# A perceiver of four layers on one core: first head reordered, scan products in pairs, one norm for two, loads ahead in portions, tails in halves

## The reference

```python
x = x + L0_xattn(ctx, layernorm(x), mask, ...)
# L0_xattn: xn = LN(ctx)*ln_x_g + ln_x_b;  ln = LN(layernorm(x))*ln_l_g + ln_l_b
#   q = ln @ Wq;  k, v = concat(xn, ln) @ Wkv
#   qn = rmsnorm(q, qn_g)/8;  kn = rmsnorm(k, kn_g);  out = softmax(mask(qn @ kn.T)) @ v @ Wout + bout
...
x = x + L1_attn(layernorm(x), ...)
# L1_attn: xn = LN(x)*ln_g + ln_b; returns x + mamba(xn) + mamba(xn reversed) reversed
# mamba: h = exp(dt*A)*h + dt*u*B ;  y = sum_n h*C + u*D     (512 inner, 16 states)
...
x = x + L2_attn(layernorm(x), ...)   # one mamba, 256 inner, 16 states
```

## Time and profile before

| | us |
|---|---|
| runs of the kernel before (3) | 2944.35 median, 2940.78 to 2949.25 |
| the profiled execution | 2943.97, span 2942.2 |
| busy in it: PE / DVE / ACT / POOL | 2679.1 / 1659.3 / 1107.9 / 610.0 |
| mean granted TensorE clock | 0.955 of full |

### The profile page before, as it was taken

How to read it: one execution, slowest core, us unless ns; L and a number is a source line. 1 busy time by engine, 2 the same in 40 slices (tenths; PEclk the granted TensorE clock), 3 DMA queues, 4 the chain that set the end, 5 groups by cost and what they waited for, 6 DMA issues and landing times. The chain is left out here.

```text
span 2942.2 us, 44133 instructions
## 1 busy us (share of the span) xinstructions
PE 2679.1 (91%) x17647; PEld 1865.4 (63%) x17647; DVE 1659.3 (56%) x3739; ACT 1107.9 (38%) x1993; POOL 610.0 (21%) x316
## 2 busy tenths in 40 slices
PE   5899999999999999689999878998996788889978
PEld 2466666666666666456767645665993467778846
DVE  5557565666666653646566555773452260067755
ACT  2343434344343432215555536651331342211123
POOL 2040403122131400000000004771001051145402
PEclk9999999999999999899999999998998899999989
DMA  4233242333324220231010001115676438643200
GB/s 156 70 82 108 69 122 75 104 97 82 97 71 109 70 60 24 86 114 46 24 46 24 2 7 34 44 40 193 242 298 247 153 95 292 216 175 134 68 16 34
DMA packets 90545, 296.06 MB, mean 101 GB/s; under 512 B 8752, under 2 KB 46326, under 8 KB 83686
## 3 DMA queue, kind: packets, MB, share of 16 engines
q1 hardware_dynamic: 86342, 284.26, 30.2%
q0 software_dynamic: 2976, 8.13, 0.8%
q10 hardware_dynamic: 1024, 0.86, 0.1%
HBM read 281.16 MB, written 11.54 MB: 99 GB/s over the span
## 5 line engine op out<-in xcount | busy, mean ns | idle before, releaser
L1923 PE MATMUL L_xattn_bank<-L_xattn_keys_tok,L_xattn_probsT 128*128 128x257 f32 x1664 | 413.3, 392 | 1.1 <-ACT L_xattn_probsT L1740 0.2
L1852 PE MATMUL L_xattn_wide<-L_xattn_keys_feat,weights_a 128*128 128x512 f32 (+2 forms) x1024 | 388.2, 522 | 4.7 <-ACT L_xattn_keys_feat L1760 3.4
L1923 PEld LDWEIGHTS L_xattn_bank<-L_xattn_keys_tok,L_xattn_probsT 128*128 128x128 f32 x1664 | 301.1, 190 | 91.2 <-issue 40.9
L1852 PEld LDWEIGHTS L_xattn_wide<-L_xattn_keys_feat,weights_a 128*128 128x128 f32 x1024 | 186.1, 192 | 152.8 <-issue 125.4
L1509 DVE COPY L_xattn_k_normed<-L_xattn_wide 128x833 f32<-128x833 f32 (+1 forms) x128 | 131.1, 1024 | 192.4 <-PE L_xattn_wide L1852 192.2
L1734 ACT ACTIVATE L_xattn_scores<-L_xattn_scores,L_xattn_neg_max 128x897 f32<-128x897 f32 x128 | 126.4, 1035 | 256.7 <-DVE L_xattn_neg_max L1534 256.7
L2868 DVE TENSOR_TENSOR_SCAN L_attn_state<-L_attn_decay,L_attn_banks 128x1024 f32<-128x1024 f32 x80 | 182.7, 2286 | 71.1 <-PE L_attn_banks L3070 71.1
L2974 POOL TENSOR_TENSOR L_attn_state<-L_attn_state,L_attn_C_rows 128x1024 f32<-128x1024 f32 x80 | 188.7, 2360 | 71.7 <-DVE L_attn_state L2868 71.6
L1529 DVE CUSTOM_DVE_ANT_0 L_xattn_scores<-L_xattn_wide,L_xattn_mask_row 128x897 f32<-128x897 f32 x128 | 134.9, 1088 | 105.9 <-issue 105.9
L3070 PEld LDWEIGHTS L_attn_banks<-L_attn_B_diagonal,L_attn_dt_u_tok 128*128 128x128 f32 x1280 | 151.1, 194 | 66.1 <-issue 64.5
L2137 DVE CUSTOM_DVE_ANT_0 L_xattn_scores<-L_xattn_banks,L_xattn_mask 128x512 f32<-128x512 f32 (+1 forms) x256 | 131.4, 569 | 92.5 <-issue 92.5
(11 more groups left out here) (522 smaller groups left out, 4714.6 us busy)
## 6 DMA issues: line engine op xcount, KB each, us to landing
L_xattn_k_scale<-L_xattn_k_scale_rows SPq DMA_DIRECT2D x128, 417.0 KB, 5.0
L_ffn_expert_w<-in_x_L_ffn SPq DMA_DIRECT2D x16, 2056.0 KB, 9.0
L_xattn_ctx_feat<-in_ctx_feat SPq DMA_DIRECT2D x20, 1601.0 KB, 8.8
L_ffn_expert_w<-in_x_L_ffn SPq DMA_DIRECT2D x17, 1024.0 KB, 5.5
L_ffn_expert_w<-in_x_L_ffn SPq DMA_DIRECT2D x15, 1028.0 KB, 5.6
L_xattn_keys_tok<-in_ctx_tok SPq DMA_DIRECT2D x8, 1536.0 KB
L_attn_C_rows<-L_attn_c_rows SPq DMA_DIRECT2D x48, 256.0 KB, 3.3
L_xattn_ctx_tok_and_one<-in_ctx_tok SPq DMA_DIRECT2D x8, 1536.0 KB
```

The costliest lines, as they stand in the source:

```text
L1852: last = nc.tensor.matmul(wide[:, 2 * h + c, 0:n], wk[:, k, p * P:(p + 1) * P], xnT[b % 2][:, k, a:a + n], start=(k == 0), stop=(k == KT - 1))
L1923: last = nc.tensor.matmul(bS[:, 0:D + 1], pT[:, c, a, :, :].rearrange("p h q -> p (h q)"), xn[b % 2][:, t, :], start=(i == 0), stop=(i == ...
```

## The change

1. **First head.** The opening block goes. L0_xattn's SP list itself loads x, the small columns of the weights, the first 690 columns of the constants, Wq, then context 0 and mask 0, and then the rest, each with its own semaphore. The columns of the weights are packed in another order. The two norms of x become one, with 1/sqrt((1+eps)v + eps²). Gain and bias of the latents are applied while the turned tensor is copied out of PSUM; the token-layout latents are gained after the query groups. The statistics of context 0 start before the query groups, its norms come in four pieces at groups 2 to 5, and PE turns the ungained context inside groups 4 to 7; gain and bias are applied in those copies. POOL spreads mask 0 first, and gains the tokens after the latents and all eight turns. SP moves the latents behind the turns.
2. **L1_attn**: one norm for two, with the same scale; the memset and x += first norm move behind.
3. **Scan loop**: two products, then two sums.
4. **L1_ffn**: the loads ahead go out in three portions, behind load(4), load(7) and load(10).
5. **Tails**: the projection is signalled by halves, the result is added by halves, the bias earlier in the loop.

```diff
-def norm_scalar(L, act, ln_stats_ready, rstd_ready, nx=0):
+def norm_scalar(L, act, ln_stats_ready, rstd_ready, twice=False):
...
+        nc.scalar.activation(rstd, L.mv[:, 2 * h:2 * h + 2, 1], ACT.Ln, scale=1.0 + EPS if twice else 1.0,
+                             bias=L.eps[:, 1:2] if twice else L.eps[:, 0:1]).then_inc(rstd_ready, 1)
...
+                L.load_first(sp, "x")
                 load_ctx(0)
                 load_mask(0)
+                L.load_first(sp, "rest")
                 sp.wait_ge(latents_ready, 1)
                 sp.dma_start(own_rows.rearrange("(t j) d -> j t d", j=2), L.z[S - 1:P:S, :, :]).then_inc(own_stored, 16)
                 sp.wait_ge(own_stored, 16)
+                sp.wait_ge(xn_turned, 8)
...
+                ctx_stats(0, range(*CTX_PIECES[0]))
...
+                norm_after = {2: range(0, 4), 3: range(4, 7), 4: range(7, 10), 5: range(10, TILES)}
                 for p in range(NQ):
...
-                    if p in (1, 2):
-                        ctx_stats(0, range(*CTX_PIECES[p - 1]))
-                    if p in (3, 4):
-                        ctx_norm(0, range(*CTX_PIECES[p - 3]))
+                    if p == 1:
+                        ctx_stats(0, range(*CTX_PIECES[1]))
+                    if p in norm_after:
+                        ctx_norm(0, norm_after[p])
+                    if p >= TURN_AFTER:
+                        keys_turned((p - TURN_AFTER) % KT, (p - TURN_AFTER) // KT)
                 q_gained(NQ - 1)
+                dve.wait_ge(w_ready[0], w_ready[1])
+                g = lambda n: w[:, at[n]:at[n] + D].unsqueeze(1).broadcast_to([P, NT, D])
+                chain(nc.vector.tensor_tensor(L.z[:, :, :], L.z[:, :, :], g("ln_l_g"), ALU.mult))
+                nc.vector.tensor_tensor(L.z[:, :, :], L.z[:, :, :], g("ln_l_b"), ALU.add).then_inc(latents_ready, 1)
...
-                dve.wait_ge(projected, 1)
-                chain(nc.vector.tensor_tensor(L.x[:, :, :], L.x[:, :, :],
-                                              wide[:, 0:2, :].rearrange("p a (b n) -> p (a b) n", n=D), ALU.add))
-                chain(nc.vector.tensor_tensor(L.x[:, :, :], L.x[:, :, :],
-                                              w[:, at["bout"]:at["bout"] + D].unsqueeze(1).broadcast_to([P, NT, D]),
-                                              ALU.add))
+                    if s == NQ:
+                        chain(nc.vector.tensor_tensor(L.x[:, :, :], L.x[:, :, :],
+                                                      w[:, at["bout"]:at["bout"] + D].unsqueeze(1).broadcast_to([P, NT, D]),
+                                                      ALU.add))
+                for half in range(2):
+                    dve.wait_ge(projected, half + 1)
+                    nc.vector.tensor_tensor(L.x[:, 2 * half:2 * half + 2, :], L.x[:, 2 * half:2 * half + 2, :],
+                                            wide[:, half, :].rearrange("p (b n) -> p b n", n=D), ALU.add)
...
+                pool.wait_ge(mask_zeroed, 1)
+                mask_row(0)
                 pool.wait_ge(w_ready[0], w_ready[1])
+                pool.wait_ge(latents_ready, 1)
+                pool.wait_ge(xn_turned, 8)
+                pool.wait_ge(mask_ready, 2)
+                gains(0, 0)
+                gains(0, 1)
...
                 project_q(0)
                 for p in range(NQ):
                     if p + 1 < NQ:
                         project_q(p + 1)
                     mean_q(p)
+                    if p >= TURN_AFTER:
+                        turn_keys((p - TURN_AFTER) % KT, (p - TURN_AFTER) // KT)
+                pe.wait_ge(L.rest_loaded, 32)
+                pe.wait_ge(w_ready[0], w_ready[1])
...
-                norm_vector(L, dve, chain, ln_stats_ready, rstd_ready, z_ready)
-                if twice:
-                    dve.wait_ge(z_ready, 2)
-                    chain(nc.vector.tensor_tensor(L.x[:, :, :], L.x[:, :, :], L.z[:, :, :], ALU.add))
-                    norm_vector(L, dve, chain, ln_stats_ready, rstd_ready, z_ready, x=L.z, z=z2, nx=1)
+                norm_vector(L, dve, chain, ln_stats_ready, rstd_ready, z_ready, z=z2)
...
+                if twice:
+                    dve.wait_ge(first_rstd_ready, 2)
+                    for t in range(NT):
+                        last = nc.vector.tensor_scalar(L.z[:, t, :], L.x[:, t, :], L.mv[:, t, 0:1], first_rstd[:, t:t + 1],
+                                                       ALU.subtract, ALU.mult)
+                    chain(last)
+                    chain(nc.vector.tensor_tensor(L.x[:, :, :], L.x[:, :, :], L.z[:, :, :], ALU.add))
...
-                for p in range(PIECES):
-                    if p + 2 < PIECES:
-                        state_input(p + 2)
-                    if p >= SPAN and p - SPAN < PC:
-                        start_y(1, p - SPAN)
...
-                    add_state(p)
+                for first in range(0, PIECES, 2):
+                    for p in (first, first + 1):
+                        if p + 2 < PIECES:
+                            state_input(p + 2)
+                    for p in (first, first + 1):
+                        if p >= SPAN and p - SPAN < PC:
+                            start_y(1, p - SPAN)
+                    for p in (first, first + 1):
...
+                        add_state(p)
...
-    AHEAD_AT = 8
+    AHEAD_AT = (4, 7, 10)
...
-                    if shared and j == AHEAD_AT:
-                        load_l2_ahead(L, sp)
+                    if shared and j in AHEAD_AT:
+                        load_l2_ahead(L, sp, AHEAD_AT.index(j))
```

More of the change, by code:

```diff
@@ L219, in turn_tensor @@
     for h in range(2):
-        if z_ready is not None:
-            pe.wait_ge(z_ready, seen + h + 1)
+        pe.wait_ge(z_ready, h + 1)
         for k in range(KT):
@@ L1460, in _ @@
                 chain(nc.vector.memset(mv[:, :, :], 1.0))
+                dve.wait_ge(zT_turned, 2)
+                for k in range(KT):
+                    nc.vector.tensor_scalar(L.zT[:, k, N // 2:N], turned_half(wide, 1)[:, k, :],
+                                            w[:, at["ln_l_gc"] + k:at["ln_l_gc"] + k + 1],
+                                            w[:, at["ln_l_bc"] + k:at["ln_l_bc"] + k + 1], ALU.mult, ALU.add
+                                            ).then_inc(zT_ready, 1)
                 for n in range(2):
@@ L1479, in q_gained, with keys_turned @@
                                                    sc[:, (p % 2) * N:(p % 2 + 1) * N], ALU.mult, ALU.mult).then_inc(q_ready, 1)
+                def keys_turned(k, x):
+                    g = 2 * x + 1
+                    a, n = KEY_GROUPS[g]
+                    dve.wait_ge(xn_turned, 4 * x + 2 * k + 2)
+                    if x == 0:
+                        nc.vector.tensor_copy(xnT[0][:, k, FIRST:FIRST + 1], L.zT[:, k, S - 1:S])
+                    cols = sum(rows(t) for t in range(a, a + n))
+                    a = key_place(a)
+                    nc.vector.tensor_scalar(xnT[0][:, k, a:a + cols], bT[:, 1, 0:cols],
+                                            w[:, at["ln_x_gc"] + k:at["ln_x_gc"] + k + 1],
+                                            w[:, at["ln_x_bc"] + k:at["ln_x_bc"] + k + 1], ALU.mult, ALU.add
+                                            ).then_inc(xT_dve, 1)
+                norm_after = {2: range(0, 4), 3: range(4, 7), 4: range(7, 10), 5: range(10, TILES)}
                 for p in range(NQ):
@@ L1815, in mean_q, with turn_keys @@
                                      ).then_inc(q_meaned, 1)
+                def turn_keys(k, x):
+                    pe.wait_ge(ctx_normed, x + 1)
+                    for g in (2 * x, 2 * x + 1):
+                        if g % 2 == 0:
+                            pe.wait_ge(xT_act, 2 * x + k)
+                        else:
+                            pe.wait_ge(xT_dve, 2 * x + k)
+                        a, n = KEY_GROUPS[g]
+                        for i in range(n):
+                            last = nc.tensor.transpose(bT[:, g % 2, i * P:(i + 1) * P], xn[0][:, a + i, k * P:(k + 1) * P],
+                                                       L.ident)
+                        last.then_inc(xn_turned, 1)
                 project_q(0)
@@ L2163, in _ @@
                     unit_taken(i)
+                    if i == 3:
+                        chain(nc.vector.tensor_tensor(L.x[:, :, :], L.x[:, :, :],
+                                                      w[:, at["bo"]:at["bo"] + D].unsqueeze(1).broadcast_to([P, NT, D]),
+                                                      ALU.add))
                 for s in range(QUADS + 1):
@@ L2807, in _ @@
                                                 ).then_inc(zT_ready, 1)
+                if KD > R:
+                    for d in range(ND):
+                        last = nc.vector.memset(dbc[d][R:KD, :], 1.0)
+                    last.then_inc(ones_ready, 1)
                 def convolve(d, m0):
@@ L2980, in _ @@
```

(6 more changed lines are left out.)

231 lines of the change are left out of this document (107 added, 124 removed).

## The result

| | us | ratio to before (95% interval) |
|---|---|---|
| changed kernel, first chip (4 runs) | 2892.55 (2889.15 to 2896.66), before 2942.84 there | 0.9826 (0.9805 to 0.9847) |
| the same again, another chip (5 runs) | 2895.22, before 2944.96 there | 0.9835 (0.9820 to 0.9850) |
| its profiled execution | span 2891.9 | |

Faster by 50 us, 1.7%; forecast 2890, range 2880 to 2911. Where it came from is read best from block to block: TensorE's first matmul of each of the twelve blocks, in the profiled executions before and after.

The account below looks back on a forecast made before the run. TensorE was taken to bound the steps and scan loop, and the chains it waits for elsewhere. 26.1 + 5.7 + 3.5 + 13.2 + 5.6 = 54.1 off 2943.97 gave 2890 us, range 2880 to 2911.

Parts of the forecast that it names:

- Head, 26.1: Opening of L0_xattn: first keys matmul at 43.5 instead of 69.62, saving 26.1 us, bounds 19 to 29.
- (a): Opening: the queries start at 10.7, 13.3 us earlier; bounds 10 to 13.5.
- (b): Opening: six blocked context norms on DVE, 7.94 us, would take 2.1, saving 5.8; bounds 0 to 5.8.
- (c): Opening: separate context turns, 6.96 us, fall away as transposes go between the last four query groups; bounds 4 to 7.
- the slow phase: Opening: first eight query matmuls stay slow at 6.67 us; three times as long puts keys at 50, none at 40.
- SP's chain late for k_scale: Opening: SP's loads before k_scale have 1 to 2 us of room; 4 us longer gives 2 to 3 back.
- The price of a meeting on DVE and POOL: Opening: a DVE instruction that meets POOL's gains takes 1.3 us in place of 0.36.
- Pairs, 13.2: Scan loop, L1_attn and L2_attn: a pair takes 5.64 instead of 6.02, 15.2 less edges of 2; bounds 0 to 15.
- Rival A: Head gives part back: slow query matmuls, DVE-POOL meetings or late k_scale; keys at 55, total 2901; chance 0.22.
- B: Scan loop: pairing gives nothing, saved changes of form being paid elsewhere; total 2903; chance 0.12.
- C: Scan loop slower than before: a pair lasts 8.34, 2.32 more, 93 us on 40 pairs; total 2996; chance 0.03.
- D: L1_ffn: a portion still delays the tokens, so the gain there is 2 to 3; total 2893; chance 0.05.

Follow-up runs that it names:

- e4: Changed kernel with the full adds behind the last matmul again in all four xattn blocks: 2902.2 us, ratio 0.9848 to the kernel before.
- e1: Changed kernel with the next block's weights and context 1 issued before SP waits for the latents: 2890.35 us, ratio 0.9808 to the kernel before.
- e8: e1 with ScalarE's copy of the own latents moved in front of the query groups: 2887.4 us, ratio 0.9800 to the kernel before.
- e6: Changed kernel with the head alone; tails, norms, pairs and loads ahead as before: 2927.66 us, ratio 0.9921 to the kernel before.
- e7: Changed kernel with three unused 128 x 1792 products on POOL, to run beside the last context norms on DVE: 2910.57 us, one run.
- e3: Changed kernel with all of L1_ffn's loads ahead issued at once behind load(8): 2901.18 us, ratio 0.9840 to the kernel before.
- e10: Changed kernel, unedited, run again on one chip beside e11: 2895.22 us, ratio 0.9835 to the kernel before.
- e9: e8 with six unused matmuls on zeros in front of TensorE's first transposes: 2889.32 us, ratio 0.9818 to the kernel before.
- e11: The kernel of e8 run again, beside e10 on one chip: 2887.78 us, ratio 0.9816 to the kernel before.
- e2: Changed kernel with one product and one sum in turn again in L1_attn and L2_attn: 2909.6 us, ratio 0.9866 to the kernel before.
- e5: Changed kernel with both norms, the memset and the add of x in front again in L1_attn: 2896.93 us, ratio 0.9826 to the kernel before.

## Why the prediction was right, and where it was off

**Head, 26.1 forecast.** The start (a), the blocked norms (b) and the separate turns (c) came as worked out, with the mask row done at 21.3, before the norms. The keys came 28.6 earlier, 2.5 more than the term. Some 1 of this is the slow phase, taken as 6.67 and measured as 5.53: in e4, where it took 6.58, the keys came at 41.95. The rest isn't broken down. What failed is the cover "SP's chain late for k_scale": its bound was 2 to 3, by way of SP's own list. The list was in time. The store that precedes k_scale goes from ScalarE's queue and moved beside 2.7 MB of loads, and took 6.25 in place of 2.75 (e1). That is 3.5 of the 4.9 lost; the rest fits the sixteen keys matmuls at 7.52 in place of the 5.83 of the kernel before and of e8. So the scaled keys came 23.7 earlier. Net, with 2.0 for the tail taken off the block's 25.0, the head gave 23, and alone, in e6, 21.4. That it came this close to 26.1 is partly luck: the keys came 2.5 earlier than summed, and that covers half of the 4.9 that the sum didn't have. The price of a meeting on DVE and POOL, 1.3 per instruction, was misread (e7): it is a whole product, 2.9 to 4.1, for each norm that meets one. No term used it.

**Tails, 5.7.** 2.0 each in L0, L1 and L3 (7.34 to 5.28 from the last projection to the next block in L1_xattn) and the clock behind it, 1.7, in L1_attn. The bias adds are hidden. L2_xattn lasts as long as before, so its 0.5 doesn't show.

**Norm in L1_attn, 3.5.** 4.95 at the first projection, 3.3 by the norm and 1.7 by the tail, in that order (e4): the term was right as a wait of 3.03, and the clock behind it needed an edit that I had counted elsewhere.

**Pairs, 13.2.** The period was right to 0.01. The gain is 8.9 and some 2.1, 11.0, because I took 6.02 from one period where the steady one is 6.00, and 2 for the edges where they cost 3: at the loop's start TensorE waits 0.59 for the scan, and at its end for POOL.

**Portions, 5.6.** The stall is gone; L1_ffn is 4.4 shorter, as its first group of matmuls took 9.85 in place of 8.62. e3 loses 8.0 without portions, 6.3 of it at the tile that waits.

**Sum.** Forecast 54.1, measured 50.3. The edited blocks give 49.5 of it. The others moved by 1.0 to 3.3 each, in both directions, and net 0.8; that they cancel is luck.

Rival A happened in part, at another place than named; B, C and D did not.

## What to carry to other kernels

When transfers are moved, look for small ones on the critical chain that will be under way in the same stretch, on whatever queue: a queue that is in time says nothing of the landing. Order matmuls of different forms so that like follows like (0.36 us per pair here), as long as the scan or whatever frees their banks keeps up. When two engines shut each other out, look at single instructions: a mean over a row mixes those that were held with those that were not. A tail that is shortened also shortens the time for which TensorE stands still, and that can change the clock of the next block's matmuls (eight warm-up matmuls at 3.67 in place of 5.37).

## What the runs showed that I had not expected

The same code of blocks that no edit touches differs from run to run by more than some of the edits are worth. L0_attn took 52.27 in the first profile of the changed kernel and 54.88 in the second, e10. Sixteen projection matmuls make most of that, first in the one and then in the other:

```profile
1159.39 3.69 PE L456 MATMUL L_attn_banks<-weights_b,z_feat 128*128 128x256 f32 x16 [0.87 <-DVE z_feat L315]
```

```profile
1159.44 5.83 PE L456 MATMUL L_attn_banks<-weights_b,z_feat 128*128 128x256 f32 x16 [0.88 <-DVE z_feat L315]
```

3.69 against 5.83, after idle times of 0.87 and 0.88. The granted clock over this stretch, up to 1170, was 1.00 and 0.79. In the other runs with halved tails the sixteen took 3.69 in e8, e9 and e11 and 5.65 to 5.84 in e1, e2, e3, e5 and e7, all behind 0.87 or 0.88; what decides it is not shown. So a few us in a total, or in one profile, tell nothing of an edit of that size; lengths of the edited block in several runs do.
